# Graph-network layer on one core: 14 copied-column tiles a round instead of 12, and one tile fetched row by row from SyncE

## Chip, core and metric

One core of one Trainium2 chip runs the whole kernel as one program. The metric is device time in microseconds (us); the time before is the median of three runs, 3641.66 us (3640.21 to 3642.67).

## The reference, cut to what matters

12,500 nodes with 128 numbers each, 400,000 edges sorted by their destination, 64 numbers on each edge.

```
h_nodes = mlp2(x, node_W1, node_b1, node_W2, node_b2)                  # 12500 x 64
h_edges = mlp2(edge_attr, edge_W1, edge_b1, edge_W2, edge_b2)          # 400000 x 64
msgs    = mlp2(concat(h_nodes[dst], h_nodes[src], h_edges), msg_W1, msg_b1, msg_W2, msg_b2)
agg     = segment_sum(msgs, dst) / max(counts, 1)
out     = layernorm(x + mlp2(concat(x, agg), upd_W1, ...)) * ln_g + ln_b
result  = layernorm(x + out)
```

`mlp2` is a linear layer, SiLU, and a second linear layer. What matters here is `h_nodes[src]`: 400,000 rows at random places. The destinations are sorted, so that side needs only short windows of consecutive rows.

## The kernel before, in words

**Node part (to about 75 us).** The second layer of the node network is folded with the message layer's weights, so that two tables of 12,500 rows of 64 float32 result, `a_table` (by destination) and `b_table` (by source), both in HBM. The hidden layer of all nodes also stays in SBUF, transposed, as `nT` (64 partitions, a column per node).

**Edge part.** A *tile* is 128 edges, a *unit* is 5 tiles (640 edges), a *round* is 25 units; there are 625 units, 25 rounds. For each unit:

- SyncE (SP in the profile) loads edge inputs into `e_ring` and destination numbers into `dst_ring`, for 4 or 5 units at a time (lines 777, 779), and the window of `a_table` for each unit (783). Every one of these waits on `second_mm`, the count of units whose second layer TensorE has done. Twice a round it reloads half of the lists of column numbers (725), once a round it loads and stores the node update's data (936, 937, 941; the store waits until VectorE is done with the update).
- GpSimd (POOL) gathers rows of `b_table` by indirect DMA, one DMA for each tile of 128 rows, into `b_ring` (line 800). The ring holds 9 unit slots: eight rotate, and the last unit of a round has the ninth. GpSimd therefore runs up to 8 units ahead; before a unit it waits for `pre_mm` of the unit 8 earlier (798).
- 12 of the 125 tiles of a round are not gathered: the last tile of each unit in `SPECIAL`. For these, 128 single columns of `nT` (64 partitions x 4 bytes) are copied into `colbuf`, each with a start address in a register: columns 0 to 57 of a tile by VectorE, 58 to 127 by ScalarE (line 632). The copies are spread evenly, 27 or 28 on VectorE and 33 or 34 on ScalarE in each unit, four units (`LEADIN`) ahead of use. Before them the engine loads the start addresses from SBUF into registers (`loaded_columns`, 617). ScalarE does this in two halves for each unit, VectorE in one. Before the first unit both make four units' worth of columns.
- TensorE: the window sums of unit i-2 (706), the second layer of unit i (686), the first layer of unit i+3 (815), then the source term: gathered tiles times an identity (692), and a copied tile times the folded weights (695).
- ScalarE: SiLU into `comb` for unit i+2 (717), first half of its columns, SiLU of the message of unit i-1 (711), second half of its columns.
- VectorE: the one-hot matrix `comb` of unit i+2 (902), `hot_ring` of unit i (891), the register load and all its columns (632), then the window sum of unit i-3 added into `agg` (912).

Once a round all engines also do a node update for 500 nodes, in pieces spread over the units 5 to 24 (`AT`): on VectorE lines 984 to 1030, on TensorE 953 to 964, on ScalarE 969. The order on each engine is the order written in the code; the engines are joined by semaphores alone.

The change touches the constants on lines 35 to 42, `b_value` (595), `load_list`/`sync_first` (722 to 739), `sync_units` (765), `pool_gathers` (793), `tensor_units` (818), `vector_units` (887), and the data layout on the host (1159).

Of the kernel before, what the change touches and what calls it, by code (L numbers as in the profile page):

```python
# [7 lines left out]
ds = bass.ds  # L8

P = 128  # L10
H = 64
D = 128
W = 64
TILES = 5
UE = TILES * P
HALF = UE // 2
ROUND = 25
# [12 lines left out]
GJ = 4  # L30
# [1 line left out]
NB = 512  # L32
EPS = 1e-5

SPECIAL = [1, 3, 5, 7, 9, 11, 13, 15, 17, 19, 21, 23]
COLS = dict(vector=58, scalar=70)
COLBUF = 4
LEADIN = 4
HALF_AT = 13
LIST_AT = (21, 8)  # L40
LOAD = dict(vector=32, scalar=40)
LISTED = 656
WORDS = 4

AT = dict(load=0, ready=2, count=3, mean=4, up=5, hidden=6, down=7, sum=8, norm1=9, affine=10, sum2=11, norm2=12,
# [10 lines left out]
def program(nc, a, out, stack):  # L56
# [7 lines left out]
    def sem(name):  # L64
        return stack.enter_context(nc.semaphore(name))
# [77 lines left out]
    for who in COLS:  # L143
# [1 line left out]
        lists[who] = to_ab[0:1, :, :, :, :].rearrange("o s t q n -> o (s t q n)").bitcast(I32)[:, at:at + words]\  # L145
            .rearrange("o (k n) -> o k n", n=LOAD[who])
        at += words
    assert at <= SR * 2 * 2 * GJ * H
    pad = sb("pad", [W, H], F32)
    rows = e_ring[0:1, :, :].rearrange("p s c -> p (s c)")  # L150
    startf, ahead = rows[:, 0:UNITS], rows[:, UNITS:2 * UNITS]
# [76 lines left out]
    a_in = [sem(f"a_in{i}") for i in range(RING)]  # L228
    b_in = [sem(f"b_in{i}") for i in range(BRING)]
    list_in = [sem(f"column_list_in{i}") for i in range(2)]  # L230
    lead_in = sem("first_columns_in")
    s_cols = sem("column_nodes_in")
    s_byte = sem("column_bytes")
# [354 lines left out]
    def b_slot(i):  # L588
        return i % BLAG if i < ROUND - 1 else BLAG

    def gathered(i):

        return [k for k in range(TILES) if not (i in SPECIAL and k == TILES - 1)]

    def b_value(r, i):

        each = [16 * len(gathered(j)) for j in range(ROUND) if b_slot(j) == b_slot(i)]
        so_far = [16 * len(gathered(j)) for j in range(i + 1) if b_slot(j) == b_slot(i)]
        return sum(each) * r + sum(so_far)

    def cols_value(who, r, i):
# [120 lines left out]
    def load_list(eng, chunk, at, n, done):  # L722

        for who in COLS:
            eng.dma_start(lists[who][:, at:at + n, :].rearrange("o k n -> o (k n)"),
                          byte_list[who][ds(chunk * LOAD[who], n * LOAD[who])].unsqueeze(0)).then_inc(done, 16)

    def sync_first(eng):
# [5 lines left out]
        load_list(eng, 0, 0, LEADIN, lead_in)  # L734
        load_list(eng, LEADIN, LEADIN, HALF_AT, list_in[0])

    def sync_last(eng):

        eng.wait_ge(list_in[0], 32 * ROUNDS + 32)

    def vector_first(eng):
# [23 lines left out]
    def sync_units(eng, base, n, step):  # L765
        for k in range(n):
            r, i = place(base, k)
            c, at = chunk_of(i)
            if at == 0:
                n = CHUNKS[c]  # L770
                first = r * (ROUND * UE) + i * UE
                here = slice(spot(i), spot(i) + n)

                wait_alone(eng, second_mm, r * ROUND + i + LEAD - CHUNKS[c - 1])
                cols = a["edgeT"][:, ds(first, n * UE)].rearrange("k (u c) -> k u c", c=UE)
                for part in range(2):
                    eng.dma_start(e_ring[part * H:(part + 1) * H, here, :], cols[:, :, part * HALF:(part + 1) * HALF])\
                       .then_inc(e_in[c % 2], 16)
                eng.dma_start(dst_ring[:, here, :].rearrange("p u c -> p (u c)"),
                              a["dst_row"][ds(first, n * UE)].partition_broadcast(H)).then_inc(d_in[c % 2], 16)  # L780
            start = next_start(eng, r, i)
            wait_alone(eng, second_mm, r * ROUND + i + 1)
            eng.dma_start(wa_ring[H:P, i % RING, :], a_table[ds(start, W), :]).then_inc(a_in[i % RING], 16)
            if i in LIST_AT:
                half = LIST_AT.index(i)
                copied = r * ROUND + LEADIN + (HALF_AT if half == 0 else 0)
                chunk, n = ((r + 1) * ROUND, HALF_AT) if half == 0 else (r * ROUND + HALF_AT, ROUND - HALF_AT)
                wait_alone(eng, col_ok["vector"], copied)
                wait_alone(eng, col_ok["scalar"], copied)
                load_list(eng, chunk + LEADIN, LEADIN + half * HALF_AT, n, list_in[half])  # L790
            step(k)

    def pool_gathers(eng, units):

        for u in units:
            r, i = divmod(u, ROUND)
            if u >= BLAG:
                wait_alone(eng, pre_mm, u - BLAG + 1)
            for k in gathered(i):
                eng.indirect_dma_start(b_ring[:, b_slot(i), k, :], None, b_table,  # L800
                                       bass.IndirectOffsetOnAxis(ap=src[:, u * TILES + k:u * TILES + k + 1], axis=0))\
                   .then_inc(b_in[b_slot(i)], 16)
# [15 lines left out]
    def tensor_units(eng, r, n, step):  # L818
        base = r * ROUND

        def sums(i):
            if i >= ADD_LAG - 1:
                wait_alone(eng, sum_ok, base + i - ADD_LAG + 3)
            else:
                wait_alone(eng, hot_ok, base + i + 1)
            eng.wait_ge(msg_ok, base + i + 1)
            window_sums(eng, i).then_inc(sum_mm, 1)

        hidden_mm(eng, r, 0)
        hidden_mm(eng, r, 1)  # L830
        eng.wait_ge(hid_ok, base + 1)
        hidden_mm(eng, r, 2)
        for i in range(n):
            rr, j = place(r, i)
            done = base + i + 1
            if i >= 2:
                sums(i - 2)
            if i < ADD_LAG + 1:
                wait_alone(eng, comb_ok, done)
            if i < 2:  # L840
                wait_alone(eng, hid_ok, done + 1)
            eng.wait_ge(a_in[j % RING], a_value(rr, j))
            for k in range(TILES):
                last = second_layer(eng, k, i)
            last.then_inc(second_mm, 1)
            if i + 3 < n:
                hidden_mm(eng, r, i + 3)
            if j in SPECIAL and i < ADD_LAG + 1:
                for who in COLS:
                    wait_alone(eng, col_ok[who], cols_value(who, rr, j))  # L850
            eng.wait_ge(b_in[b_slot(j)], b_value(rr, j))
            source_term(eng, i, j, b_slot(j)).then_inc(pre_mm, 1)
            step(i)
        for i in (n - 2, n - 1):
            sums(i)
# [31 lines left out]
    def vector_units(eng, r, n, step):  # L887
        base = r * ROUND

        def hot_of(i):  # L890
            eng.tensor_tensor(hot_ring[:, i % HOTS, :, :],  # L891
                              dst[:, ds((base + i) * TILES, TILES)].bitcast(F32).unsqueeze(2).to_broadcast([P, TILES, W]),
                              p_iota.unsqueeze(1).to_broadcast([P, TILES, W]), ALU.is_equal).then_inc(hot_ok, 1)

        def comb_of(i):
            rr, j = place(r, i)
            c, at = chunk_of(j)
            if at == 0:
                wait_alone(eng, d_in[c % 2], chunk_value(rr, c, 16))
            if i >= COMBS:  # L900
                wait_alone(eng, second_mm, base + i - COMBS + 1 + LEAD)
            eng.scalar_tensor_tensor(comb[H:P, i % COMBS, :], dst_ring[:, spot(j), :], win_from[:, ds(base + i, 1)],  # L902
                                     p_row.to_broadcast([H, UE]), ALU.subtract, ALU.is_equal).then_inc(comb_ok, 1)

        def add_sums(i):
            rr, j = place(r, i)
            u = base + i
            start = next_start(eng, rr, j)
            eng.wait_ge(sum_mm, u + 1)
            window = agg[0:H + 1, ds(start, W)]  # L910
            wait_alone(eng, sum_ok, u + 1)
            eng.tensor_tensor(window, window, sums_of(i), ALU.add).then_inc(sum_ok, 1)  # L912

        for i in range(AHEAD):
            comb_of(i)
        for i in range(n):
            rr, j = place(r, i)
            if i + AHEAD < n:
                comb_of(i + AHEAD)
            hot_of(i)  # L920
            if j in (0, HALF_AT):
                wait_alone(eng, list_in[j // HALF_AT], 32 * rr + 32)
            starts_v = loaded_columns(eng, "vector", j + LEADIN)
            copied_columns(eng, "vector", eng.tensor_copy, j + LEADIN, starts_v).then_inc(col_ok["vector"], 1)
            if i >= ADD_LAG:
                add_sums(i - ADD_LAG)
            step(i)
        for i in range(n - ADD_LAG, n):
            add_sums(i)
# [122 lines left out]
    def pool_general(eng):  # L1052
        a_table_stored(eng)
        for u in range(EARLY):
            eng.wait_ge(b_in[b_slot(u)], 16 * len(gathered(u)))
        with eng.Fori(0, UNITS) as u:
            wait_alone(eng, gen["in"], 64 * u + 64)
            for k in range(TILES):
# [100 lines left out]
def _laid_out(inputs):  # L1159
# [9 lines left out]
    for k in ("src", "dst"):  # L1169
        d[k] = g[k].reshape(-1, P).T  # L1170
    d["dst_row"] = g["dst"].reshape(-1)
    special = g["src"].reshape(-1, ROUND, TILES, P)[:, SPECIAL, TILES - 1, :]
    chunks = special.shape[0] * ROUND
    for who, (first, last) in dict(vector=(0, COLS["vector"]), scalar=(COLS["vector"], P)).items():
# [21 lines left out]
```

## Time and profile before

| | before |
|---|---|
| median of 3 runs | 3641.66 us |
| the profiled execution | 3643.69 us |
| its span, first to last instruction | 3641.8 us |
| POOL busy | 2698.5 us (74%) |
| ACT busy | 2995.1 us (82%) |
| PE busy | 2794.5 us (77%) |
| DVE busy | 2735.3 us (75%) |
| mean granted TensorE clock | 0.76 |
| DMA engines busy, in the edge part | 0.4 to 0.5 |

PE is TensorE, DVE VectorE, ACT ScalarE, POOL GpSimd, SP SyncE. No engine is busy for more than 82% of the span. "Idle before, releaser" in a row of the profile is the time that the engine stood idle ahead of such instructions and what ended it; "issue" means that the profile shows nothing it waited for, so that its own sequencer was at work. Busy time doesn't count register, branch, semaphore and DMA-issuing instructions.

### The profile page before, as it was taken

How to read it: one execution, taken by the hardware profiler on the slowest of the kernel's cores; microseconds unless marked ns; L12 is line 12 of the kernel's file. 1: busy time of each engine (PE TensorE's matmuls, PEld its weight loads, DVE VectorE, ACT ScalarE, POOL GpSimd, SP SyncE). 2: the span in 40 equal slices, each digit the busy share in tenths (PEclk: the TensorE clock that was granted, in tenths of full speed). 3: DMA queues.
4: the chain of work that ended last, by engine and by line, in shares of the span. 5: the costliest groups of instructions: out<-in, count | busy, mean ns of one | idle time of the engine just before them, and what ended most of it. 6: DMA issues, size and time to landing. Idle time of an engine off the chain costs nothing.

```text
span 3641.8 us, 93892 instructions
## 1 busy us (share of the span) xinstructions
PE 2794.5 (77%) x16224; PEld 2174.9 (60%) x16224; DVE 2735.3 (75%) x20847; ACT 2995.1 (82%) x23073; POOL 2698.5 (74%) x2848
## 2 busy tenths in 40 slices
PE   4878778777877788787777778777777787887785
PEld 2666556555666566666655556565655565665564
DVE  4778778778678677777687787786787877777876
ACT  3998888888888888888888888888888888888885
POOL 4777777777777777777777777777777777777774
PEclk7777777778777777777687787777777777677776
DMA  7444444444444444444454444444444444444442
GB/s 218 95 100 98 86 91 95 94 101 95 92 98 87 92 100 91 98 101 87 88 103 86 100 95 94 97 89 89 101 91 98 101 88 93 88 94 100 95 94 44
DMA packets 257330, 350.11 MB, mean 96 GB/s; under 512 B 105688, under 2 KB 193069, under 8 KB 246862
## 3 DMA queue, kind: packets, MB, share of 16 engines
q1 hardware_dynamic: 163340, 245.92, 31.8%
q0 software_dynamic: 91424, 95.97, 14.3%
q14 instruction: 481, 3.94, 0.4%
q8 instruction: 131, 2.15, 0.3%
q10 hardware_dynamic: 1954, 2.14, 0.2%
HBM read 330.76 MB, written 13.01 MB: 94 GB/s over the span
## 4 chain that ended last, share of the span: by engine, by line
POOL 64%; issue 21%; PE 8%; DMA 4%; DVE 2%; ACT 0%; DVEq 0%; SPq 0%; POOLq 0%; ACTq 0%
POOL b_ring L800 64%; DMA b_ring<-b_table,src 4%; PE p_pre L686 2%; PE p_pre L692 2%; PE p_sum L706 1%; PE p_hid L815 1%; DVE colbuf L632 1%; DMA work<-in_xT 1%; PE p_pre L695 0%; DVE comb L902 0%; PE p_last L958 0%; PE p_hid L378 0%; PE p_last L959 0%; DMA b_table<-to_ab 0%; DVE stats L995 0%
## 5 line engine op out<-in xcount | busy, mean ns | idle before, releaser
L800 POOL DMA_INDIRECT b_ring<-b_table,src x2825 | 2676.1, 947 | 865.8 <-issue 850.2
L632 ACT COPY colbuf<-shared 64x4 uint8 x21134 | 2128.0, 190 | 152.1 <-issue 140.7
L632 DVE COPY colbuf<-shared 64x4 uint8 x17511 | 1375.4, 194 | 282.2 <-issue 275.6
L686 PE MATMUL p_pre<-wa_ring,comb 128*128 128x64 f32 x6250 | 1027.7, 325 | 0.0
L686 PEld LDWEIGHTS p_pre<-wa_ring,comb 128*128 128x128 f32 x6250 | 979.2, 241 | 1.0 <-issue 1.0
L692 PE MATMUL p_pre<-b_ring,ident 128*128 128x320 f32 (+1 forms) x1250 | 575.3, 552 | 490.8 <-DMA b_ring<-b_table,src 488.3
L717 ACT ACTIVATE comb<-p_hid,b_e 64x320 f32<-64x320 f32 x1250 | 652.8, 522 | 359.8 <-PE p_hid L815 346.4
L902 DVE SCALAR_TENSOR_TENSOR comb<-shared,p_const 64x640 f32<-64x640 int32 x625 | 554.1, 887 | 506.2 <-PE p_pre L686 420.8
L706 PEld LDWEIGHTS p_sum<-hot_ring,msg 128*65 128x65 f32 x6250 | 579.8, 178 | 476.5 <-DVE agg L912 280.7
L706 PE MATMUL p_sum<-hot_ring,msg 128*65 128x64 f32 x6250 | 641.3, 267 | 278.4 <-DVE agg L912 171.6
L692 PEld LDWEIGHTS p_pre<-b_ring,ident 128*128 128x128 f32 x1250 | 295.5, 250 | 691.1 <-DMA b_ring<-b_table,src 577.2
L815 PE MATMUL p_hid<-e_ring,w_e 128*128 128x320 f32 x1250 | 592.3, 562 | 20.4 <-DMA e_ring<-in_edgeT 11.5
L711 ACT ACTIVATE msg<-p_pre 128x320 f32<-128x320 f32 x625 | 273.5, 438 | 68.0 <-PE p_pre L695 42.5
L891 DVE TENSOR_TENSOR hot_ring<-dst,p_const 128x320 f32<-128x320 f32 x625 | 304.7, 488 | 19.7
L815 PEld LDWEIGHTS p_hid<-e_ring,w_e 128*128 128x128 f32 x1250 | 235.8, 235 | 21.8 <-DMA e_ring<-in_edgeT 11.6
L695 PEld LDWEIGHTS p_pre<-w_ab,colbuf 64*128 64x128 f32 x600 | 112.3, 233 | 137.6 <-issue 137.6
L695 PE MATMUL p_pre<-w_ab,colbuf 64*128 64x64 f32 x600 | 159.4, 354 | 0.0
L912 DVE TENSOR_TENSOR agg<-agg,p_sum 65x64 f32 x625 | 135.2, 216 | 10.4 <-PE p_sum L706 7.9
L985 DVE RECIPROCAL p_last<-p_last 64x500 f32<-64x500 f32 x25 | 82.1, 3283 | 0.9
L964 PEld LDWEIGHTS p_last<-w_u,work 65*125 65x125 f32 x200 | 48.6, 320 | 4.3 <-ACT work L969 2.4
L964 PE MATMUL p_last<-w_u,work 65*125 65x128 f32 x200 | 47.1, 379 | 0.8 <-ACT work L969 0.8
L958 PE MATMUL p_last<-work,w_ux 128*64 128x500 f32 x50 | 41.7, 932 | 5.3 <-DVE work L987 5.3
(106 smaller groups left out, 592.4 us busy)
## 6 DMA issues: line engine op xcount, KB each, us to landing
e_ring<-in_edgeT SPq DMA_DIRECT2D x250, 320.0 KB
shared<-in_dst_row SPq DMA_DIRECT2D x125, 640.0 KB
b_ring<-b_table,src POOLq DMA_INDIRECT x2825
e_ring<-in_edgeT SPq DMA_DIRECT2D x50, 400.0 KB
shared<-in_dst_row SPq DMA_DIRECT2D x25, 800.0 KB
wa_ring<-a_table SPq DMA_DIRECT2D x625, 16.0 KB
work<-in_xT SPq DMA_DIRECT2D x25, 250.0 KB
work<-in_x SPq DMA_DIRECT2D x25, 250.0 KB
```

Source lines behind the costliest of these rows:

```text
L632: end = copy(colbuf[:, special % COLBUF, at:at + 1].bitcast(U8), of[j])
L686: return eng.matmul(p_pre[:, i % 2, k * H:(k + 1) * H], comb[:, i % COMBS, k * P:(k + 1) * P], wa_ring[:, i % RING, :], start=k == 0, stop ...
L692: last = eng.matmul(p_pre[:, i % 2, 0:n * H], ident[:, :], b_ring[:, slot, 0:n, :].rearrange("p k n -> p (k n)"), start=False, stop=n == T ...
L695: last = eng.matmul(p_pre[:, i % 2, n * H:(n + 1) * H], colbuf[:, SPECIAL.index(j) % COLBUF, :], w_ab[0:H, H:2 * H], start=False, stop=True)
L706: last = eng.matmul(sums_of(i), msg[:, i % 2, k, :], hot_ring[:, i % HOTS, k, :], start=k == 0, stop=k == TILES - 1)
L711: return eng.activation(msg[:, i % 2, :, 0:H], of, ACT.Silu)
L717: last = eng.activation(comb[0:H, i % COMBS, part * HALF:(part + 1) * HALF], p_hid[rows, bank, 0:HALF], ACT.Silu, bias=b_e1[rows, :])
L800: eng.indirect_dma_start(b_ring[:, b_slot(i), k, :], None, b_table, bass.IndirectOffsetOnAxis(ap=src[:, u * TILES + k:u * TILES + k + 1], ...
L815: eng.matmul(p_hid[:, i % 2, 0:HALF], w_e1[:, :], e_ring[:, spot(j), :], start=True, stop=True)\
L891: eng.tensor_tensor(hot_ring[:, i % HOTS, :, :], dst[:, ds((base + i) * TILES, TILES)].bitcast(F32).unsqueeze(2).to_broadcast([P, TILES, W ...
L902: eng.scalar_tensor_tensor(comb[H:P, i % COMBS, :], dst_ring[:, spot(j), :], win_from[:, ds(base + i, 1)], p_row.to_broadcast([H, UE]), AL ...
L912: eng.tensor_tensor(window, window, sums_of(i), ALU.add).then_inc(sum_ok, 1)
```

## The change

The number of copied-column tiles of a round goes from 12 to 14, with seven column buffers in place of four, and VectorE makes 61 of the 128 columns of a tile and ScalarE 67. One further tile of a round, tile 3 of unit 24, leaves GpSimd's list: SyncE fetches it with 128 single-row DMAs, 8 in each of the units 7 to 22, with row numbers that it loads into registers from a list in SBUF. TensorE waits for these rows at unit 24. VectorE's columns of a unit are made in two halves, one right behind `comb`, one behind the window sum; `hot_ring` and the window sum come between them.

```
-SPECIAL = [1, 3, 5, 7, 9, 11, 13, 15, 17, 19, 21, 23]
-COLS = dict(vector=58, scalar=70)
-COLBUF = 4
+SPECIAL = [1, 2, 4, 6, 8, 9, 11, 13, 15, 17, 18, 20, 22, 24]
+COLS = dict(vector=61, scalar=67)
+COLBUF = 7
-LOAD = dict(vector=32, scalar=40)
+LOAD = dict(vector=40, scalar=40)
+ROW_TILE = (24, 3)
+ROWS_A_STEP = 8
+ROWS_FROM = 7
...
+    def by_pool(i):
+        return [k for k in gathered(i) if (i, k) != ROW_TILE]
...
+    def load_rows(eng, r):
+        eng.dma_start(row_list, a["rows"][ds(r * P, P)].unsqueeze(0)).then_inc(row_list_in, 16)
+
+    def fetch_rows(eng, r, i):
+        first = (i - ROWS_FROM) * ROWS_A_STEP
+        if first == 0:
+            wait_alone(eng, row_list_in, 16 * r + 16)
+        _, nodes = nc.values_load_multi_w_load_instructions(
+            row_list[:, first:first + ROWS_A_STEP], engines=[eng.engine], min_val=0, max_val=N - 1,
+            skip_runtime_bounds_check_because="an edge's source is a node")
+        unit, tile = ROW_TILE
+        for q, node in enumerate(nodes):
+            eng.dma_start(b_ring[first + q:first + q + 1, b_slot(unit), tile, :], b_table[ds(node, 1), :])\
+               .then_inc(row_in[q % len(row_in)], 16)
+        if first + ROWS_A_STEP == P:
+            load_rows(eng, r + 1)
...
     sync_units, behind the list loads and ahead of step(k):
+            if 0 <= i - ROWS_FROM < P // ROWS_A_STEP:
+                fetch_rows(eng, r, i)
...
     pool_gathers:
-            for k in gathered(i):
+            for k in by_pool(i):
...
     tensor_units, ahead of the wait on b_in:
+            if j == ROW_TILE[0]:
+                for arrived in row_in:
+                    wait_alone(eng, arrived, (rr + 1) * (16 * P // len(row_in)))
...
     vector_units:
-            hot_of(i)
             if j in (0, HALF_AT):
                 wait_alone(eng, list_in[j // HALF_AT], 32 * rr + 32)
-            starts_v = loaded_columns(eng, "vector", j + LEADIN)
-            copied_columns(eng, "vector", eng.tensor_copy, j + LEADIN, starts_v).then_inc(col_ok["vector"], 1)
+            starts_v = loaded_columns(eng, "vector", j + LEADIN, 0, 2)
+            copied_columns(eng, "vector", eng.tensor_copy, j + LEADIN, starts_v, 0, 2)
+            hot_of(i)
             if i >= ADD_LAG:
                 add_sums(i - ADD_LAG)
+            starts_v = loaded_columns(eng, "vector", j + LEADIN, 1, 2)
+            copied_columns(eng, "vector", eng.tensor_copy, j + LEADIN, starts_v, 1, 2).then_inc(col_ok["vector"], 1)
```

## Rows read from the trace of the kernel before

**Rows 1.** The page: busy time by engine, and the chain that ended last

```profile
PE 2794.5 (77%) x16224; PEld 2174.9 (60%) x16224; DVE 2735.3 (75%) x20847; ACT 2995.1 (82%) x23073; POOL 2698.5 (74%) x2848
...
POOL 64%; issue 21%; PE 8%; DMA 4%; DVE 2%; ACT 0%; DVEq 0%; SPq 0%; POOLq 0%; ACTq 0%
```

**Rows 2.** Groups by line: busy us, mean ns; idle before them, releaser

```profile
L800 POOL DMA_INDIRECT b_ring<-b_table,src x2825 | 2676.1, 947 | 865.8 <-issue 850.2
L632 ACT COPY colbuf<-shared 64x4 uint8 x21134 | 2128.0, 190 | 152.1 <-issue 140.7
L632 DVE COPY colbuf<-shared 64x4 uint8 x17511 | 1375.4, 194 | 282.2 <-issue 275.6
```

**Rows 3.** The gather's line: duration ns min/median/max, first and last start

```profile
L800 POOL DMA_INDIRECT b_ring<-b_table,src x2825: 944/944/1484, 66.2 to 3601.6; - x189
```

**Rows 4.** Who waited for whom: total us, times, longest us

```profile
PE p_pre L692 <- DMA b_ring<-b_table,src: 488.3, 149, 8.5
DVE comb L902 <- PE p_pre L686: 420.8, 185, 8.3
ACT comb L717 <- PE p_hid L815: 346.4, 192, 5.8
DVE comb L902 <- DMA shared<-in_dst_row: 68.6, 29, 3.9
```

**Rows 5.** Stretches of a round's length: busy us (instructions) of each engine

```profile
1592.00:1733.00 141.00, 110.29 (x638) 85.35 (x638) 108.44 (x835) 119.61 (x930) 106.59 (x113) 0.78 0.47 95
3140.00:3282.00 142.00, 115.51 (x641) 89.17 (x640) 108.69 (x838) 119.54 (x923) 107.58 (x114) 0.74 0.47 96
```

**Rows 6.** VectorE in order of time: start, us, line; idle before

```profile
1594.26 0.89 DVE L902 SCALAR_TENSOR_TENSOR comb<-shared,p_const 64x640 f32<-64x640 int32 x1
1595.18 0.49 DVE L891 TENSOR_TENSOR hot_ring<-dst,p_const 128x320 f32<-128x320 f32 x1
1595.58 2.14 DVE L632 COPY colbuf<-shared 64x4 uint8 x28
...
1597.87 0.89 DVE L902 SCALAR_TENSOR_TENSOR comb<-shared,p_const 64x640 f32<-64x640 int32 x1
...
1608.33 0.89 DVE L902 SCALAR_TENSOR_TENSOR comb<-shared,p_const 64x640 f32<-64x640 int32 x1 [1.59 <-PE p_pre L686]
...
1610.37 2.32 DVE L632 COPY colbuf<-shared 64x4 uint8 x27 [0.63 <-issue]
```

**Rows 7.** VectorE making the columns ahead of the first unit, in halves

```profile
78.09 1.29 DVE L632 COPY colbuf<-shared 64x4 uint8 x16 [4.76 <-issue]
79.85 0.87 DVE L632 COPY colbuf<-shared 64x4 uint8 x11 [0.46 <-issue]
81.58 1.30 DVE L632 COPY colbuf<-shared 64x4 uint8 x16 [0.85 <-issue]
```

**Rows 8.** ScalarE in order of time, one unit without a wait

```profile
1628.65 1.05 ACT L717 ACTIVATE comb<-p_hid,b_e 64x320 f32<-64x320 f32 x2
1629.73 2.00 ACT L632 COPY colbuf<-shared 64x4 uint8 x20
...
1632.08 1.42 ACT L632 COPY colbuf<-shared 64x4 uint8 x14
1633.40 1.05 ACT L717 ACTIVATE comb<-p_hid,b_e 64x320 f32<-64x320 f32 x2
```

**Rows 9.** SyncE's issues by line: duration ns min/median/max

```profile
L725 SPq DMA_DIRECT2D to_ab<-bytes_for_scalar x52: 219/231/326, 75.5 to 3562.4; - x52
```

**Rows 10.** SyncE's window loads, 64 rows each

```profile
L783 SPq DMA_DIRECT2D wa_ring<-a_table x625: 468/480/548, 79.3 to 3579.5; - x157
```

**Rows 11.** The waits of SyncE's queue: total us, times, longest us

```profile
SPq L783 <- PE p_pre L686: 2066.7, 486, 13.0
```

**Rows 12.** TensorE's second layer of one unit at either granted clock

```profile
1585.15 1.28 PE L686 MATMUL p_pre<-wa_ring,comb 128*128 128x64 f32 x10
...
1594.41 2.34 PE L686 MATMUL p_pre<-wa_ring,comb 128*128 128x64 f32 x10
```

More of the change, by code:

```diff
@@ L147, in program @@
         at += words
-    assert at <= SR * 2 * 2 * GJ * H
+    row_list = to_ab[0:1, :, :, :, :].rearrange("o s t q n -> o (s t q n)").bitcast(I32)[:, at:at + P]
+    assert at + P <= SR * 2 * 2 * GJ * H
     pad = sb("pad", [W, H], F32)
@@ L230, in program @@
     list_in = [sem(f"column_list_in{i}") for i in range(2)]
+    row_list_in = sem("row_list_in")
+    row_in = [sem(f"rows{q}_in") for q in range(4)]
     lead_in = sem("first_columns_in")
@@ L593, in gathered @@
         return [k for k in range(TILES) if not (i in SPECIAL and k == TILES - 1)]
+    def by_pool(i):
+        return [k for k in gathered(i) if (i, k) != ROW_TILE]
     def b_value(r, i):
-        each = [16 * len(gathered(j)) for j in range(ROUND) if b_slot(j) == b_slot(i)]
-        so_far = [16 * len(gathered(j)) for j in range(i + 1) if b_slot(j) == b_slot(i)]
+        each = [16 * len(by_pool(j)) for j in range(ROUND) if b_slot(j) == b_slot(i)]
+        so_far = [16 * len(by_pool(j)) for j in range(i + 1) if b_slot(j) == b_slot(i)]
         return sum(each) * r + sum(so_far)
@@ L735, in sync_first @@
         load_list(eng, LEADIN, LEADIN, HALF_AT, list_in[0])
+        load_rows(eng, 0)
+    def load_rows(eng, r):
[13 more added lines that the diff above has]
+            load_rows(eng, r + 1)
     def sync_last(eng):
+        eng.wait_ge(row_list_in, 16 * ROUNDS + 16)
         eng.wait_ge(list_in[0], 32 * ROUNDS + 32)
@@ L1054, in pool_general @@
         for u in range(EARLY):
-            eng.wait_ge(b_in[b_slot(u)], 16 * len(gathered(u)))
+            eng.wait_ge(b_in[b_slot(u)], 16 * len(by_pool(u)))
         with eng.Fori(0, UNITS) as u:
@@ L1171, in _laid_out @@
     d["dst_row"] = g["dst"].reshape(-1)
+    rows = g["src"].reshape(-1, ROUND, TILES, P)[:, ROW_TILE[0], ROW_TILE[1], :]
+    d["rows"] = np.concatenate([rows, np.zeros_like(rows[0:1])]).reshape(-1)
     special = g["src"].reshape(-1, ROUND, TILES, P)[:, SPECIAL, TILES - 1, :]
```

## The prediction, as it was put on record before the kernel was run

> **What bounds the kernel now.** I read the page first. No engine is busy for more than 82%, so busy time doesn't name the bound; the chain that ended last does, with 64% POOL and 21% "issue" [rows 1]. The groups by line say what that issue time is: 850.2 of POOL's 865.8 us of idle time ahead of the gathers is its own [rows 2]. A gather takes 944 ns at least and in the median [rows 3], and 2825 of them fill the time from 66.2 to 3601.6 us: 3535.4 / 2824 = 1.2519 us from start to start. POOL never stands still, and everybody else waits for it: TensorE 488 us for gathered rows, VectorE 421 and ScalarE 346 us for TensorE [rows 4]. A round is 113 gathers, 113 x 1.2519 = 141.5 us, which is 5.66 us a unit. About 40 us of span follow the last gather's start, and the profiled execution (3643.69) is 1.9 us over its span and 2.0 us over the median; I carry differences over to the median.
>
> So the rate of GpSimd sets the time, and the question is how far below 141.5 us a round the others can go.
>
> **GpSimd: what goes.** 14 copied tiles and the row tile leave 125 - 15 = 110 gathers a round: 110 x 1.2519 = 137.7 us. 75 gathers fewer in all: 75 x 1.2519 = 93.9 us. If nothing else changes the median becomes 3641.7 - 93.9 = 3547.8. That is the floor.
>
> **VectorE: what comes.** Copies a round go from 58 x 12 = 696 to 61 x 14 = 854. One costs 1375.4 / 17511 = 78.5 ns [rows 2]: 158 x 78.5 ns = 12.4 us a round. A round's stretch has 108.5 us of VectorE's busy time now [rows 5], so 121 then. To this comes idle time that isn't a wait for others. First the small gaps between its instructions, which I estimate at 3 us: of 906 us of idle time in the span, 490 are the two waits in [rows 4] and 276 the register loads in [rows 2]; of the 140 left about half lies in the edge part. Second the register loads, 275.6 / 25 = 11 us a round now. In one unit that VectorE enters without having waited, the load is hidden altogether (28 copies start at 1595.58, under the end of `hot_ring`); after a wait for TensorE it shows as 0.63 us [rows 6], since the sequencer has no work queued in front of it.
>
> After the change there are two loads a unit. The one behind `comb` has 0.89 us of `comb` over it in place of 0.89 + 0.49, but fetches 20 numbers in place of 28; the second, 16 numbers, has the last copies, `hot_ring` (0.49) and the window sum over it. The bounds for both together: nothing, if they hide as at 1595.58; and in the columns made ahead of the first unit, where copies alone cover them, 0.46 us ahead of 11 copies and 0.85 us ahead of 16 [rows 7], 1.3 us a unit. I take 0.45 us: half of the units enter after a wait and show some 0.6 on the first load, the others nothing, and the second shows 0.15. 25 x 0.45 = 11 us. The sum is 121 + 3 + 11 = 135 us a round against GpSimd's 137.7. VectorE fits, with 2.7 us to spare where it had 141.5 - 122.5 = 19. With the bounds it is 124 to 156.
>
> One rule bears on this. The Trainium skill, "Advanced Engine Details and Errata", section Engine Queue Depths, gives VectorE and ScalarE a queue of 8 instructions. By it the sequencer can be 8 copies ahead, which is 8 x 78.5 = 0.63 us of cover for a load behind copies; by the row alone the second load, behind copies, `hot_ring` and the sum, would be covered as 28 numbers were at 1595.58. By the rule the second load would still show 0 to 0.3 us, by the row nothing. The gap of 0.46 us ahead of 11 copies [rows 7] is in keeping with a cover that is limited.
>
> **ScalarE.** Copies a unit go from 70 x 12 / 25 = 33.6 to 67 x 14 / 25 = 37.5. A unit without a wait took 4.75 us with 34 [rows 8], 100 ns a copy (2128.0 us / 21134, [rows 2]): 4.75 + 0.35 = 5.10 us, 128 a round with the update's single SiLU. That is under 137.7, the cover being waits of 14 us a round (346 / 25) now. It is worth nothing by itself, but ScalarE at 5.10 can no longer pull the group of three engines forward when it has fallen behind.
>
> **TensorE.** Two more small source terms a round, about a microsecond; its second layer takes 2.34 us at the lower granted clock and 1.28 at the higher [rows 12]. After each long wait it goes at the lower clock (1.2 of 2.4 GHz), where a whole unit takes it about as long as GpSimd gives it (sums, layers and source term in the ratio of these rows, an estimate of 5.5 to 6 us). Now VectorE and ScalarE have room to make up for that; then they hardly have. GpSimd's lead of 8 units lets the three lag some units without cost, so only a lasting lack counts. The earlier window sum helps: TensorE gets `agg` half a unit sooner. The four waits at unit 24 cost at most what a wait that is already met costs; the last rows are issued about six units (33 us) earlier.
>
> **SyncE.** 128 issues a round. The trace shows no single-row DMA from a register. From below it is the load of one long row, 0.231 us [rows 9]; from above the window load, 64 rows from a register, 0.480 us [rows 10]. I take 0.35, nearer to the one-row case with a register move added: 8 x 0.35 = 2.8 us, and half a microsecond or so for 8 registers, 3.3 us in 16 of 25 units. SyncE waits 2066.7 / 625 = 3.3 us a unit at line 783 alone [rows 11], so the period holds it. Behind these issues stand the window load of the next unit, five units ahead of use, and the chunk loads (lines 777 and 779), which are two units ahead: VectorE already waited 68.6 us for destination rows, 29 times [rows 4]. In a period of 5.5 us SyncE is back before the next one is due: nothing. From 0.57 us an issue on it is not (8 x 0.57 + 0.9 = 5.5).
>
> **Start and end.** The lead-in columns grow from 27.8 to 34.2 a unit, four units: from [rows 7] (3.5 us for 27 columns) some 3 us more on VectorE. GpSimd has filled 8 slots by then and covers it. At the end, what the three engines lag behind comes after the last gather. I add 8 us for that and 12 us, 0.5 a round, for places where the lag runs over the ring. Forecast: 3547.8 + 20 = **3568**, own range 3548 to 3600.
>
> **Rivals.**
> (a) VectorE becomes the bound, and the kernel is slower. Place: the two register loads. A round is 124 us plus 25 loads' gaps; with 0.85 us a unit (both loads bare after each wait) it is 145, and 25 x (145 - 141.5) = 88 us on top: 3730. It decides from (141.5 - 124) / 25 = 0.70 us a unit on. For it: 0.46 to 0.85 us in [rows 7]. Against: that stretch has only copies as cover.
> (b) The same with 0.55 to 0.70 us: VectorE sets the pace, but below the old one. At 0.62, 139.5 us a round: 3642 - 50 = 3592, with the end's lag 3600.
> (c) SyncE is too slow. At 0.65 us an issue, 6.1 us a unit, the chunk loads come up to 4 us late, four of six in a round; a third of it lands on the path: 25 x 5 = 125, 3690.
> (d) GpSimd's gathers get slower as VectorE copies more. If each added copy held GpSimd off for its 78.5 ns, a round would be 137.7 + 12.4 = 150: 3642 + 215 = 3857. Against it, the gather takes 944 ns in the minimum and in the median while VectorE is 75% busy, half of that with these copies. The Trainium skill says so in "SBUF — State Buffer" in its part on doors: a VectorE copy in a two-port mode locks GpSimd out while it writes descriptors. These rows show no such lock for copies of 4 bytes.
> (e) The change gives nothing: the lag of the three engines eats the 94 us by coupling (no single engine over 137.7), 3630 to 3650.
>
> **How the numbers follow.** Forecast 0.50; (b) 0.20; (a) 0.16; (c) 0.05; (d) 0.01; (e) 0.08. A change of 0.2% (7 us) is about what a measurement can tell. Faster: 0.50 + 0.20 and a part of (e), 0.73; within 0.2%: 0.06; slower: 0.21. The range reaches from just under the floor, 3545, to 3650, and leaves out most of (a), (c) and (d).
>
> **What would show it.** Right: 2750 gathers, start to start 1.25 us still, issue most of their idle time; the chain still mostly POOL. VectorE's wait for TensorE down from 421 us to under 150; its issue time ahead of the copies 200 to 350 us; ScalarE's waits near 200. Single rows at 0.3 to 0.4 us. Wrong: POOL's idle time ended by TensorE for tens of microseconds (then the others are the bound), an issue time ahead of VectorE's copies over 430 us, gathers over 944 ns in the median, or waits for destination rows above 100 us.

## The result, and the profile after

The changed kernel takes 3695.52 us (median of 4 runs, 3691.98 to 3696.43) against 3641.15 for the kernel before (four runs, the three named above among them): a ratio of 1.0147, 95% interval 1.013 to 1.0165. It is slower by 54 us where 73 us less were forecast. The span of its profiled execution is 3690.1 us, 48 us over the 3641.8 before. Rival (a), VectorE as the bound, happened.

The page of the changed kernel, busy time by engine and the chain of waits, answers to [rows 1]:

```profile
PE 2940.0 (80%) x16324; PEld 2288.2 (62%) x16324; DVE 3122.9 (85%) x24822; ACT 3249.4 (88%) x25539; POOL 2624.6 (71%) x2773
...
DVE 75%; issue 11%; DVEq 10%; ACT 3%; PE 1%; DMA 1%; SPq 0%; ACTq 0%
```

POOL has left the chain; it was 64% of it. In its place stands VectorE with 75%, and with 10% "DVEq", VectorE's sequencer. The groups by line and the gather's own durations answer to [rows 2] and [rows 3]:

```profile
L834 POOL DMA_INDIRECT b_ring<-b_table,src x2750 | 2602.6, 946 | 952.8 <-issue 811.3
L642 ACT COPY colbuf<-shared 64x4 uint8 x23600 | 2370.4, 189 | 105.4 <-issue 90.5
L642 DVE COPY colbuf<-shared 64x4 uint8 x21486 | 1742.6, 191 | 452.1 <-issue 427.3
```

```profile
L834 POOL DMA_INDIRECT b_ring<-b_table,src x2750: 942/944/1240, 61.6 to 3610.8; - x197
```

The 75 gathers are gone and a gather still takes 944 ns, with 3975 more copies on VectorE: rival (d) is out. But POOL now stands idle for TensorE, and TensorE for VectorE. The waits, which answer to [rows 4]:

```profile
PE p_sum L716 <- DVE agg L949: 463.2, 254, 6.9
DVE colbuf L642 <- issue: 427.3, 1031, 5.1
ACT comb L727 <- PE p_hid L849: 256.0, 122, 6.1
...
POOL b_ring L834 <- PE p_pre L705: 121.5, 61, 6.1
```

VectorE's wait for TensorE ahead of `comb`, 421 us before, is 1.1 us now: the group of three engines turned round, and VectorE hardly waits for anybody. The list by line has it in one row (idle ahead of VectorE's `comb`, by what ended it):

```profile
L939 DVE SCALAR_TENSOR_TENSOR comb<-shared,p_const 64x640 f32<-64x640 int32 x625 | 554.0, 887 | 26.9 <-DMA shared<-in_dst_row 5.5 <-PE p_pre L696 1.1
```

A stretch of a round's length (busy us and instructions of PE, PEld, DVE, ACT, POOL), as [rows 5]; one from 2000 us on has 122.99 for VectorE:

```profile
1500.00:1643.00 143.00, 119.31 (x647) 93.85 (x647) 122.32 (x988) 128.70 (x1020) 104.67 (x112) 0.70 0.46 93
```

From `comb` to `comb`, the 23 rounds after the first take 143.0 us on average, against 141.5 before. VectorE is busy for 122 to 123 of them; 427.3 / 25 = 17 us are issue time ahead of its copies, the rest, some 3 us, the small gaps between instructions.

The 48 us between the two profiled executions are therefore not 25 times one number: 23 rounds at 1.42 us make 33, the first round (131.3 us for 118.7, of which VectorE waited only 14 for others) 12.6, the last one 7.6, and start and end give 4.5 back.

### The profile page after: what moved, and what is told of

Read it like the earlier page. It is cut to its first block, busy times and chain, and to the rows that moved or that the text cites. A ratio compares the mean times of both kernels' runs of the same rounds, so it can differ in the third digit from the quotient of the medians.

```text
span 3690.1 us, 112417 instructions
## 1 busy us (share of the span) xinstructions
PE 2940.0 (80%) x16324; PEld 2288.2 (62%) x16324; DVE 3122.9 (85%) x24822; ACT 3249.4 (88%) x25539; POOL 2624.6 (71%) x2773
## 4 chain that ended last, share of the span: by engine, by line
DVE 75%; issue 11%; DVEq 10%; ACT 3%; PE 1%; DMA 1%; SPq 0%; ACTq 0%
DVE colbuf L642 42%; DVE comb L939 13%; DVEq L627 6%; DVE hot_ring L928 6%; DVEq L639 3%; DVE p_last L1024 2%; ACT colbuf L642 2%; DVE agg L949 2%; DVE stats L1034 1%; DVE p_last L1050 1%; DVE half L1044 1%; DVE half L1045 1%; DVE rstd L1046 1%; DVE work L1050 1%; DVE mv L1037 1%
## 5 line engine op out<-in xcount | busy, mean ns | idle before, releaser
L834 POOL DMA_INDIRECT b_ring<-b_table,src x2750 | 2602.6, 946 | 952.8 <-issue 811.3
L642 ACT COPY colbuf<-shared 64x4 uint8 x23600 | 2370.4, 189 | 105.4 <-issue 90.5
L642 DVE COPY colbuf<-shared 64x4 uint8 x21486 | 1742.6, 191 | 452.1 <-issue 427.3
L696 PE MATMUL p_pre<-wa_ring,comb 128*128 128x64 f32 x6250 | 1080.0, 337 | 0.0
L696 PEld LDWEIGHTS p_pre<-wa_ring,comb 128*128 128x128 f32 x6250 | 1025.7, 251 | 1.0 <-DVE comb L939 0.6
L849 PE MATMUL p_hid<-e_ring,w_e 128*128 128x320 f32 x1250 | 669.9, 629 | 28.5 <-DMA e_ring<-in_edgeT 18.0
L702 PEld LDWEIGHTS p_pre<-b_ring,ident 128*128 128x128 f32 x1250 | 330.5, 265 | 172.4 <-issue 123.6
L849 PEld LDWEIGHTS p_hid<-e_ring,w_e 128*128 128x128 f32 x1250 | 263.4, 260 | 31.5 <-DMA e_ring<-in_edgeT 19.8
L705 PEld LDWEIGHTS p_pre<-w_ab,colbuf 64*128 64x128 f32 x700 | 134.0, 238 | 169.0 <-issue 169.0
L705 PE MATMUL p_pre<-w_ab,colbuf 64*128 64x64 f32 x700 | 189.6, 360 | 0.0
```

What stands on the lines that cost most here:

```text
L642: end = copy(colbuf[:, special % COLBUF, at:at + 1].bitcast(U8), of[j])
L696: return eng.matmul(p_pre[:, i % 2, k * H:(k + 1) * H], comb[:, i % COMBS, k * P:(k + 1) * P], wa_ring[:, i % RING, :], start=k == 0, stop ...
L702: last = eng.matmul(p_pre[:, i % 2, 0:n * H], ident[:, :], b_ring[:, slot, 0:n, :].rearrange("p k n -> p (k n)"), start=False, stop=n == T ...
L705: last = eng.matmul(p_pre[:, i % 2, n * H:(n + 1) * H], colbuf[:, SPECIAL.index(j) % COLBUF, :], w_ab[0:H, H:2 * H], start=False, stop=True)
L849: eng.matmul(p_hid[:, i % 2, 0:HALF], w_e1[:, :], e_ring[:, spot(j), :], start=True, stop=True)\
```

## Where a unit's time goes on VectorE

One unit of VectorE in the changed kernel, in order of time (start, us, line, count, idle before):

```profile
1533.43 0.89 DVE L939 SCALAR_TENSOR_TENSOR comb<-shared,p_const 64x640 f32<-64x640 int32 x1
1534.49 1.55 DVE L642 COPY colbuf<-shared 64x4 uint8 x20 [0.17 <-issue]
1536.06 0.49 DVE L928 TENSOR_TENSOR hot_ring<-dst,p_const 128x320 f32<-128x320 f32 x1
1536.47 0.21 DVE L949 TENSOR_TENSOR agg<-agg,p_sum 65x64 f32 x1
1536.97 1.08 DVE L642 COPY colbuf<-shared 64x4 uint8 x14 [0.30 <-issue]
1538.09 0.89 DVE L939 SCALAR_TENSOR_TENSOR comb<-shared,p_const 64x640 f32<-64x640 int32 x1
```

4.66 us, though nothing is waited for. The sequencer's side is in the rows of its register loads: min/median/max in ns, for the changed kernel and for the kernel before. I had not read the latter row for the prediction.

```profile
L627 DVEq TENSOR_LOAD <-to_ab x1258: 1094/1347/1766, 72.5 to 3652.1; - x180
```

```profile
L617 DVEq TENSOR_LOAD <-to_ab x633: 849/1850/1883, 76.8 to 3595.0; - x159
```

A load of 16 numbers takes about 1.10 us, of 20 1.35, of 28 1.85: some 62 ns for each further number. The sequencer's operations that prepare six copies (`lower_ap`), four of them for 20 copies here, start 0.31 us apart:

```profile
L639 DVEq FUSED_REGOPS  x4: 53/93/93, 1534.4 to 1535.3; - x4
```

That is 52 ns for the dispatch of a copy. In the whole trace 93% of the distances between two such operations are 0.33 us or less, so this pace is the sequencer's usual one. The engine, when copies stand ready, starts one every 71 ns (median over all copies). So a further column costs the sequencer 0.115 us and the engine 0.071.

In the unit shown the sequencer has no idle time. Its first load starts at 1532.95 and ends at 1534.32, the second runs from 1535.69 to 1536.79, the next unit's first starts at 1537.65, and the time between them is filled with dispatch. In sum: 1.37 + 1.10 us for the loads, 34 x 0.052 = 1.8 for the copies, and the remaining 0.4 to 0.5 for `comb`, `hot_ring`, the window sum, their waits and register operations make the 4.70 us from load to load. In every fourth unit a load of window starts comes on top (0.35 us). The engine's own work in that unit is 4.2 us, the 4.66 less the two gaps of 0.17 and 0.30. Over all 480 units without a piece of the update the distance from `comb` to `comb` is 4.94 us; the 144 with one take 8.17. (480 x 4.94 + 144 x 8.17) / 624 = 5.69 us a unit, where GpSimd gives one every 5.51.

SyncE's row fetch is harmless, though dearer than reckoned. A single row from a register takes 225 ns and with its register operations 0.41 us from start to start, 3.3 us for eight. The load of eight row numbers takes 0.96 us in the median, where half a microsecond was taken; together 4.25 us in the median, for 3.3 in the sum, and still less than a unit's 5.5.

```profile
L763 SPq DMA_DIRECT2D b_ring<-b_table x3200: 217/225/288, 106.0 to 3616.8; - x189
```

## The experiments

**The first set: no comparison.** In this set the kernel before itself took 4679.43 us in place of 3641. The edits of the four kernels are shown with their repeats below.

> The changed kernel with the row tile given back to GpSimd (111 gathers a round; SyncE fetches no rows, TensorE has no wait for them). Theory: VectorE's sequencer is the bound (two register loads a unit of 1.35 and 1.10 us, 34 copies at 0.052 us, the rest 0.5 to 0.7), a round takes 143 us whatever GpSimd does; GpSimd's own need becomes 111 x 1.2519 = 139.0 us, still less. So the time stays at 3695, within 10 us, and GpSimd's wait for TensorE falls by about the 1.25 us a round. Rival, that the row fetch delays SyncE or TensorE: the time falls by more than 30 us, at best to 3548 + 31 = 3579.

> The changed kernel without VectorE's second register load of a unit: the second half of its columns is copied from the first half's addresses (so these columns are the wrong nodes), as many copies as before. Theory: the sequencer needs 4.94 - 1.10 = 3.8 us a unit, less than the 4.3 us that the engine executes; a round is 25 x 4.4 + 18.6 = 129 us, GpSimd's 137.7 sets the pace again: 3555 to 3590, and VectorE waits for TensorE again by more than 100 us. Rival, that the copies themselves or the coupling of the engines is what costs: over 3650.

> The kernel before with the row tile alone: 12 copied tiles, 58 and 70 columns, one register load a unit, order as before; GpSimd gathers 112 tiles a round. Theory: GpSimd stays the bound and one gather less a round is worth 25 x 1.2519 = 31 us: 3610, within 6. Rival, that SyncE's 128 issues (3.1 us in 16 of 25 units) make the chunk loads late or the wait at unit 24 costs: 3630 or more, and VectorE waits for destination rows above 100 us.

> The changed kernel with VectorE making 57 of the 128 columns and ScalarE 71. Theory: 2.24 columns a unit less at 0.062 us of load and 0.052 us of dispatch each, 0.26 us a unit, 6.4 us a round: VectorE's round 143.4 - 6.4 = 137.0, just under GpSimd's 137.7; ScalarE's busy time 128.7 + 5.6 = 134.3. Time 3550 to 3600. Rival, that three engines near their limit hold each other up however the columns are split: 3640 to 3695, with TensorE's and ScalarE's waits for each other grown.

They took 4709, 4835, 4879 and 4990 us, ratios of 1.006, 1.032, 1.043 and 1.067. None of the numbers of the theories was tested. The row tile alone, for instance, showed idle time ahead of VectorE's copies that the same kernel doesn't have elsewhere (301 us in its repeat):

```profile
DVE colbuf L642 <- issue: 814.8, 1316, 7.3
```

**The second load left out.** This was the test of the theory: take away one register load and nothing else. The second half of the columns is then copied from the addresses of the first, so the kernel leaves out the right nodes there, but not a single copy.

```
-            starts_v = loaded_columns(eng, "vector", j + LEADIN, 1, 2)
             copied_columns(eng, "vector", eng.tensor_copy, j + LEADIN, starts_v, 1, 2).then_inc(col_ok["vector"], 1)
```

> The changed kernel without VectorE's second register load of a unit: the second half of its columns is copied from the first half's addresses (these columns are the wrong nodes), as many copies as before. Theory, if the kernel before is at 3641: the sequencer needs 4.94 - 1.10 = 3.8 us a unit, less than the 4.3 us that the engine executes; GpSimd's 137.7 us a round set the pace again: 3555 to 3590, and VectorE waits for TensorE by more than 100 us. Rival, that the copies themselves or the coupling of the engines is what costs: over 3650.

3557.53 us, ratio 0.9772 (0.9754 to 0.979). The same 21,486 copies, the same row tile, the same order; 625 loads of about 1.10 us less, and 138 us less time than the changed kernel's. The page and the waits of that kernel:

```profile
PE 2898.5 (82%) x16324; PEld 2263.3 (64%) x16324; DVE 3064.0 (86%) x24822; ACT 3245.7 (91%) x25539; POOL 2627.2 (74%) x2773
...
ACT 40%; DVE 27%; PE 12%; SPq 6%; issue 6%; DMA 3%; DVEq 2%; ACTq 2%
```

```profile
DVE colbuf L642 <- issue: 216.8, 336, 5.0
```

The issue time ahead of the copies halves, VectorE's busy time falls by 2% (3123 to 3064), and the time comes within 10 us of GpSimd's floor of 3548. VectorE waits for TensorE by 93 us, a little under the 100 expected, since ScalarE is next in line: 40% of the chain.

**The row tile alone**, on the kernel before (`SPECIAL`, `COLS`, `COLBUF` and the order of VectorE's work as before):

```
-            for k in gathered(i):
+            for k in by_pool(i):
     with fetch_rows in sync_units and the four waits in tensor_units, as in the change
```

> The kernel before with the row tile alone again (12 copied tiles, one register load a unit, order as before; GpSimd gathers 112 tiles a round), because in the first set the kernel before itself took 4679 us in place of 3641, with idle time between instructions on every engine that the profile calls issue. Theory, if the kernel before is back at 3641: GpSimd stays the bound and one gather less a round is worth 25 x 1.2519 = 31 us: 3610, within 6. Rival, that SyncE's 128 issues cost: 3630 or more. If the kernel before is at 4680 again, neither is tested, and the row tile costs some per cent as in the first set (4879).

3614.89 us, ratio 0.9928 (0.9912 to 0.9945): 26 us less, where 25 gathers at 1.2519 are 31. The row tile works, and nearly at its full price. VectorE's wait for TensorE is 336 us there (in an execution of 3633.40, the slowest of five): the slack is still present.

**The row tile taken back** from the changed kernel (`by_pool` returns `gathered(i)`; no `fetch_rows`, no waits for it):

> The changed kernel with the row tile given back to GpSimd (111 gathers a round; SyncE fetches no rows, TensorE has no wait for them). Theory: VectorE's sequencer is the bound, GpSimd's need of 139.0 us is still under 143: the time stays at 3695, within 10 us, and GpSimd's idle time ended by TensorE falls from 136 us to about 105. Rival, that the row fetch is what costs: more than 30 us less, at best 3579.

3693.99 us, ratio 1.0145 (1.0128 to 1.0162), the changed kernel's own. One gather a round more costs nothing and one less gives nothing, once VectorE is the bound. GpSimd's idle time ended by TensorE went from 136 to 105 us, as the sum had it. Its chain:

```profile
DVE 72%; issue 10%; DVEq 9%; ACT 4%; PE 2%; DMA 1%; ACTq 0%; SPq 0%
```

**57 and 71 columns** in place of 61 and 67:

```
-COLS = dict(vector=61, scalar=67)
+COLS = dict(vector=57, scalar=71)
```

> The changed kernel with VectorE making 57 of the 128 columns and ScalarE 71. Theory: VectorE's sequencer saves 2.24 columns at 0.115 us, 0.26 us a unit, 6.4 us a round: 143.4 - 6.4 = 137.0, just under GpSimd's 137.7; ScalarE's busy time a round rises from 128.6 to 134.2 and it had some 8 us of idle time in a round of 137 without the second load. So 3560 to 3620, with ScalarE in the chain. Rival, that moving columns doesn't matter since the coupling costs: 3680 to 3700. If ScalarE becomes the bound at once: above 3640.

3642.42 us, ratio 1.0007 (0.9997 to 1.0016). 52 us faster than 61 and 67, but 22 us above the expected range and, by the expectation's own words, where ScalarE as the bound would put it; a run further down tests that. The chain and the waits:

```profile
ACT 41%; DVE 31%; PE 12%; issue 7%; DVEq 4%; ACTq 2%; SPq 2%; DMA 1%
```

```profile
PE p_sum L716 <- ACT msg L721: 361.9, 261, 2.5
...
PE p_sum L716 <- DVE agg L949: 213.3, 118, 6.1
...
DVE comb L939 <- PE p_pre L696: 92.9, 94, 2.0
```

No one engine has the chain to itself: TensorE's window sums wait now for ScalarE's message, now for VectorE's sum. VectorE's round is 140.4 us, of which 136.0 are its own (busy, issue and small gaps; 137.0 was expected) and 4.4 are waits for others.

**The same split with one load** of 32 numbers and the order of before (`comb`, `hot_ring`, load, all copies, window sum). (One load of 36 numbers, for 61 columns, wasn't run.)

> The same split of 57 and 71, with VectorE's one register load a unit (32 numbers) and the order of the kernel before. Two loads of 16 take 2 x 1.10 = 2.2 us, one of 32, by 1.85 for 28 and 1.35 for 20, some 2.1. Theory, that the sequencer's sum counts and not the number of the loads nor where they stand: within 20 us of the split with two loads. Rival, that the two halves are the mistake: 40 us or more below it. Rival, that the earlier window sum of the halves helps TensorE: 20 us or more above it.

3649.94 us, ratio 1.0024 (1.0013 to 1.0036), 8 us above the two halves. Two loads of 16 take about as long as one of 32 (2.20 us against a median of 2.10), and cut and order together make little difference: it is the sum of numbers loaded and copies that counts. Cut and order were not varied one by one.

**57 and 71 without the second load.** Which of the two engines holds the split at 3642? A first try fell into a set in which the kernel before took 4698 us (4960, ratio 1.056), together with one of the next kernel (4897, ratio 1.042).

> The split of 57 and 71 in two halves, and VectorE without its second register load of a unit (the second half of its columns is copied from the first half's addresses, so these are the wrong nodes). It asks what holds the 57/71 split at 3642. Theory: ScalarE is the bound there (135.7 us busy in 143, 41% of the chain); then VectorE's relief gives little, 3620 to 3645. Rival, that VectorE's sequencer is still half of it and the two hold each other up: 3560 to 3600, with VectorE's issue time ahead of the copies down from 362 us to about 150.

> Again, the kernel before having taken 4698 us in the last set: the split of 57 and 71 in two halves, VectorE without its second register load of a unit (the second half of its columns is copied from the first half's addresses, so these are the wrong nodes). What holds the 57/71 split at 3642? Theory: ScalarE (135.7 us busy in 143, 41% of the chain); then VectorE's relief gives little, 3620 to 3645. Rival, that VectorE's sequencer is still half of it and the two hold each other up: 3560 to 3600.

3577.28 us where the kernel before took 3660.91 in that set: ratio 0.9773 (0.974 to 0.9806). Against the split's 1.0007 that is 0.023 of 3641, some 85 us, off by VectorE's relief alone. VectorE's issue time ahead of its copies falls from 362 to 171 us. My theory, ScalarE as the bound at 3642, is wrong, and the time is in the rival's range: VectorE's sequencer is on the path there. That ScalarE is on it as well, so that the two hold each other up, is read from the chain (41% ACT, 31% DVE) and not shown: no run relieves ScalarE alone. Without VectorE's second load ScalarE is next in line, busy for 95% of the span:

```profile
PE 2910.3 (81%) x16324; PEld 2279.4 (64%) x16324; DVE 2975.5 (83%) x23413; ACT 3375.8 (95%) x26948; POOL 2647.8 (74%) x2773
```

**13 copied tiles and the row tile**, 58 and 70 columns, one load:

```
+SPECIAL = [1, 3, 5, 7, 9, 11, 13, 14, 16, 18, 20, 22, 24]
+COLBUF = 13
```

> 13 copied tiles and the row tile: 58 and 70 columns, 13 column buffers, one register load a unit and the order of the kernel before; GpSimd gathers 111 tiles a round. Theory: GpSimd needs 139.0 us a round; VectorE's sequencer (3.9 us a unit with 27.8 columns, 0.115 us for each further column) 4.2 us a unit, 124 us a round with the update; so GpSimd sets the pace: 3642 - 50 x 1.2519 = 3579, up to 3590. Rival, that each added tile already costs more coupling than it saves GpSimd: above the 3615 of the row tile alone.

3585.43 us, ratio 0.9848 (0.9832 to 0.9865). It leaves nothing of the computation out and beats both kernels, 55 us under the one before and 110 under the changed one; of the kernels run that leave nothing out it is the fastest. It stands 6 us above GpSimd's 3579, and its chain is spread over everybody:

```profile
POOL 24%; DVE 19%; PE 18%; ACT 15%; issue 13%; DMA 5%; SPq 3%; DVEq 2%; ACTq 1%
```

Its waits show that a long issue time alone doesn't make an engine the bound. It is nearly as long as in the changed kernel (427.3), but here VectorE still waits for TensorE, since its own round is 130 us (111.3 busy, 16.2 issue, 2.8 small gaps) against GpSimd's 139:

```profile
DVE colbuf L642 <- issue: 409.1, 575, 4.7
...
DVE comb L939 <- PE p_pre L696: 132.8, 115, 4.0
```

**The same with the two halves:**

> 13 copied tiles (58 and 70 columns) and the row tile as in the run of 3585 us, but with VectorE's columns in two halves as in the change (loads of 16 and 16 numbers; one-hot matrix and window sum between them). Theory: VectorE's sequencer needs 31.7 us less a round than its 143 for 14 tiles only in the columns (30.2 in place of 34.2 a unit, 0.46 us, 11.5 us a round), 132 against GpSimd's 139.0: the time stays within 10 us of 3585. Rival, that halves cost by themselves: above 3605. Rival, that the earlier window sum helps where VectorE isn't the bound: under 3575, which GpSimd's floor of 3579 hardly allows.

> Again: 13 copied tiles (58 and 70 columns) and the row tile as in the run of 3585 us, but with VectorE's columns in two halves as in the change. Theory: VectorE's round is 143 - 11.5 = 132 against GpSimd's 139.0; the time stays within 10 us of 3585. Rival, that halves cost by themselves: above 3605. Rival, that the earlier window sum helps: under 3575.

In the later set 3602.91 us, with the kernel before at 3660.91: ratio 0.9847 (0.981 to 0.9883), equal to the 0.9848 of one load. Where VectorE isn't the bound, the halves neither cost nor help by more than that interval, some 13 us to either side. ("31.7 us less" in the first of the two expectations is a slip: the difference is the 11.5 us that give its 132.)

## Why the prediction was wrong, step by step

- **What bounds the kernel before**: right. The row tile alone and the 13 tiles follow GpSimd's count at 1.2519 us a gather to some 6 us.
- **GpSimd's part, -93.9 us**: right as a need (2750 gathers, 944 ns), and reached only where VectorE was relieved (3557.5).
- **VectorE's busy time**, 121 us a round: 122.5. Nearly right, as were the small gaps, 3.2 for 3.
- **The register loads, 0.45 us a unit: this step failed.** Measured 427.3 / 625 = 0.68, so that VectorE's round became 122.5 + 16.6 + 3.2 = 142.3 (142.5 from `comb` to `comb`, all rounds) in place of 121 + 11 + 3 = 135, against GpSimd's 137.7. The 0.68 is within the bounds (0 to 1.3) and just under the 0.70 from which rival (a) was to decide; with the measured busy time and gaps that point lies at (141.5 - 125.7) / 25 = 0.63. The size was off because the step's picture was: I treated a load as a latency that other work covers, and asked how much showed. It is sequencer time that adds up. Loads and dispatch take the sequencer 4.7 us in the unit shown, the engine's work 4.2, and then no queue of instructions helps: cover works only while the sequencer gets ahead, and with 28 numbers and 28 copies it could (3.6 us from `comb` to `comb` without a gap, [rows 6], and 4.4 on average after a wait, against 5.66 from GpSimd). The price of an added column is 0.115 us, not the 0.0785 that [rows 2] gives; for 6.3 columns a unit that is 0.72 us, not 0.5. The 0.23 us a unit between 0.68 and 0.45 are nearly 6 us a round, against 2.7 to spare.
- **The rule on queues of 8** instructions (the Trainium skill, "Advanced Engine Details and Errata", Engine Queue Depths) was read as a limit on the cover of one load. The gap of 0.30 us ahead of the second half at 1536.97 is in keeping with the 0 to 0.3 that it gave. It doesn't ask whether the sequencer can fill the queue at all, and that decided here.
- **ScalarE** at 5.10 us a unit: right, 128.7 us busy a round against 128. **TensorE**: what its lower clock costs by itself no run here separates. **SyncE**: no cost, as forecast, though eight rows took 4.25 us in place of 3.3; the chunk loads were not late (5.5 us of waits for destination rows).
- **Start and end, coupling**: 20 us were added for it. In the changed kernel, where VectorE sets the pace, it can't be told apart. It was too small where all engines are near their limit: 57 and 71 columns should have come to GpSimd's pace by each engine's own sum and stayed some 85 us above what VectorE's relief then gave.
- **Rivals**: (a) had the bound, the place and the side, with 3730 for 3695, but at 0.85 us a unit in place of 0.68; it had 0.16. The sign set for it, over 430 us of issue time ahead of VectorE's copies, just failed to show (427.3) and is a poor one, as the 409.1 of the 13 tiles tell; POOL's 136 us of idle time ended by TensorE is the sign that did show. (c) is refuted by the row tile alone and taken back, (d) by the gather's 944 ns. (e), coupling without a single engine over its limit, is not what happened at 61 columns, but the 57/71 split looks like it.

## What to carry to other kernels

Where an engine runs many short instructions with addresses from registers, add up its sequencer's time as for a second engine: register loads and register operations have rows of their own in the trace, and idle time called "issue" that vanishes after a lead is not proof that it is covered. Compare the sums, not the idle time called issue. Price an added instruction by the larger of the two, and ask which engine is second before relieving the first: of the splits run here the thirteenth tile was the last that paid, and the fourteenth moved the bound. When several engines come within 3% of each other, as at 57 and 71 columns, allow for their waiting in turn: it took 2% there.

## What was not expected of the hardware

In two of the sets the kernel before took 4679 and 4698 us in place of 3641, in every one of its runs. The record gives the first of these sets and the last one, in which it took 3661, the same chip number, 7; whether that is one and the same chip it doesn't say, so it isn't shown that the slowness belongs to a chip. With the row tile alone, the gather's and the copies' median durations are the same as in its repeat to 1% (948 ns for 956, 157 for 157). What grows is idle time: called issue, 815 us for 301 ahead of VectorE's copies and 707 for 154 ahead of ScalarE's, while GpSimd's falls (667 for 838) and its waits for TensorE rise (14 to 1079). The kernel before had a mean granted TensorE clock of 0.61 to 0.64 there, for 0.74 to 0.76. In these sets every kernel with the row fetch was 3 to 7% slower than the kernel before, the one without it 0.6%, and with the row tile alone SyncE's queue has 43% of the chain: there the row fetch does cost, much as rival (c) had it. The cause of the idle time stays open: no run here separates it.

Loading numbers from SBUF into registers costs about 62 ns for each further one on VectorE, whether in one piece or two, and about as much on ScalarE (1.26 us for 20).
